# A decoder block with two cross attentions: row products 22 slots ahead over three banks, turned maxima in single precision, and a last stage that centres x in PSUM by ScalarE

## The reference

```
x = x + tanh(g_xattn[0]) * wkv(layernorm(x), context)                 # a recurrence
x = x + tanh(g_ffn[0])   * one-bit feed-forward(layernorm(x))         # 512 -> 2048 -> 512
x = x + tanh(g_xattn[1]) * attention(layernorm(x), context)           # 16 heads of 32
x = x + tanh(g_ffn[1])   * ternary projection(layernorm(x))           # RMS norm, int8 activations
```

```
q = qdq(x) @ qdq(wq).T + bq ;  k, v = split(context @ wkv.T + bkv)
attn = softmax(q k^T / sqrt(32)) ;  o = attn v ;  out = qdq(o) @ qdq(wp).T + bp
```

## Time and profile before

| what | value |
|---|---|
| median of 3 runs | 1025.7 us (1024.91 to 1027.72) |
| the profiled execution | 1025.1 us, span 1023.4 us |
| PE busy | 832.3 us, 81% |
| DVE busy | 794.2 us, 78% |
| ACT busy | 560.1 us, 55% |
| POOL busy | 489.6 us, 48% |
| attention, first to last score product | 624.6 to 899.8 us |

### The profile page before, as it was taken

How to read it: one execution, slowest core, us unless ns; L and a number is a source line. 1 busy time by engine, 2 the same in 40 slices (tenths; PEclk the granted TensorE clock), 3 DMA queues, 4 the chain that set the end, 5 groups by cost and what they waited for, 6 DMA issues and landing times.

```text
span 1023.4 us, 15702 instructions
## 1 busy us (share of the span) xinstructions
PE 832.3 (81%) x4423; PEld 362.5 (35%) x4423; DVE 794.2 (78%) x1524; ACT 560.1 (55%) x993; POOL 489.6 (48%) x556
## 2 busy tenths in 40 slices
PE   1289889828999999999999956989989898854554
PEld 1245445403444454444454421222222222222221
DVE  3949899857898999998998655677777778427995
ACT  2358888734455565665655543555555555544441
POOL 1185665212344443445433444475756666536561
PEclk9569999969999999999999957999999999977776
DMA  8538987622333323233233331212122120000111
GB/s 283 190 96 217 220 205 200 179 57 42 62 73 62 62 52 62 52 71 62 51 62 63 72 96 40 75 51 71 55 62 64 56 68 2 1 0 9 53 41 61
DMA packets 165159, 84.45 MB, mean 83 GB/s; under 512 B 116960, under 2 KB 149872, under 8 KB 165104
## 3 DMA queue, kind: packets, MB, share of 16 engines
q1 hardware_dynamic: 165104, 83.81, 32.5%
HBM read 37.50 MB, written 12.58 MB: 49 GB/s over the span
## 4 chain that ended last, share of the span: by engine, by line
PE 50%; DVE 15%; issue 6%; SPq 3%; ACT 3%; POOL 1%; DMA 0%; DVEq 0%; ACTq 0%; POOLq 0%
PE bank L1002 20%; PE bank L1011 10%; PE bank L1099 5%; DVE B L1529 4%; PE bank L1072 4%; PE bank L1089 4%; SPq L412 3%; PE bank L1109 2%; ACT A L852 1%; DVE B L1536 1%; PE bank L1111 1%; DVE B L1622 1%; PE bank L1029 1%; DVE B L1624 1%; POOL B L609 1%
## 5 line engine op out<-in xcount | busy, mean ns | idle before, releaser
L1002 PE MATMUL bank<-A,B 128*128 128x512 f16 x1024 | 233.0, 381 | 18.6 <-DMA B<-B 14.8
L1529 DVE TENSOR_REDUCE B<-bank 128x1 f32<-128x512 f32 x256 | 163.5, 685 | 71.2 <-PE bank L1072 69.9
L852 ACT ACTIVATE A<-bank 128x512 f32<-128x512 f32 x256 | 138.8, 592 | 88.7 <-PE bank L1089 86.3
L525 POOL TENSOR_TENSOR B<-B 128x512 f16<-128x512 f32 x64 | 75.5, 1179 | 207.1 <-ACT B L740 154.2
L1002 PEld LDWEIGHTS bank<-A,B 128*128 128x128 f16 x1024 | 100.3, 98 | 141.5 <-issue 18.3
L598 POOL TENSOR_TENSOR B<-A 128x512 f32<-128x512 f32 x64 | 79.3, 1268 | 112.8 <-ACT A L852 112.8
L1011 PE MATMUL bank<-A,B 128*128 128x512 f16 x512 | 120.7, 379 | 0.0
L1072 PE MATMUL bank<-A 96*128 96x512 f16 x256 | 100.9, 405 | 15.3 <-DVE B L1529 10.3
L735 ACT ACTIVATE bank<-B 128x512 f32<-128x512 f32 x64 | 38.5, 602 | 124.2 <-DVE B L1424 123.9
L1089 PE MATMUL bank<-A 98*128 98x512 f16 x256 | 96.5, 391 | 11.3 <-DMA A<-B 6.6
L598 POOL TENSOR_TENSOR B<-B,A 128x512 f32<-128x512 f32 x64 | 79.1, 1269 | 0.0
(11 more groups left out here) (232 smaller groups left out, 1546.5 us busy)
## 6 DMA issues: line engine op xcount, KB each, us to landing
B<-in_L_ffn_w_dram SPq DMA_DIRECT2D x48, 256.0 KB, 3.5
A<-k_parts SPq DMA_DIRECT2D x48, 128.0 KB, 2.5
A<-B SPq DMA_DIRECT2D x192, 32.0 KB, 1.9
X<-in_x_dram SPq DMA_DIRECT2D x4, 1024.0 KB, 13.6
B<-in_ctx_dram SPq DMA_DIRECT2D x16, 256.0 KB, 5.3
k_parts<-B SPq DMA_DIRECT2D x16, 256.0 KB, 4.7
v_rows<-B SPq DMA_DIRECT2D x16, 256.0 KB, 3.2
B<-v_rows SPq DMA_DIRECT2D x16, 256.0 KB, 3.2
```

What stands on the lines that cost most here:

```text
L525: nc.gpsimd.tensor_tensor(HLb[j][:, 1, :], Db[j % 2], HLb[j][:, 0, :], ALU.subtract).then_inc(lo_done, 1)
L852: nc.scalar.activation(PR[(HG * t + j) % 8], bank[2 + j % 2][:, :], ACT.Exp, scale=SCALE).then_inc(exp_done, 1)
L1002: last = mm(bank[2 * n + q][:, :], XQT[a][:, m, :], wt[:, m % DB, j * 512:j * 512 + 512], start=(m == 0), stop=(m == 2 * DB - 1))
L1529: reduce(NMX[:, t, j:j + 1], bank[n % 2][:, :], AX.X, ALU.max, negate=True).then_inc(row_max, 1)
```

## The change

In the attention:

- Row products run 22 slots ahead of the scores instead of one group (`LEAD` 6 more), over three banks 0, 1 and 5 instead of two. The list `ROWS` says how many stand in each slot, and `coming` which ones. Before the first group 22 of them run instead of 16.
- The maxima are turned in single precision straight from `NMX` (now two buffers) into 4 rows of bank 4, so `max_parts` goes. ACT's copy makes the high half-precision part in `CT[0]`, and a new DVE operation `c_low` takes bank 4 minus that for the low part `CT[1]`. `send_c` waits for both.
- `c_turn` moves from the middle of slots 12 to 15 to slot 9, ACT's `c_out` to after exponential 10, `c_low` to slot 12 of DVE's list.
- `sums_out` moves from DVE to ACT, after exponential 5. `ot_out` moves from before exponential 0 to after exponential 3. `sum_weights` is cut in two: the four products over the last block of exponentials (`sum_last`) come first, in slot 2, those over `ACC` in slot 3. `sum_turn` is in slot 6, `o_turn` in slot 7 and now into bank 7.
- PE and DVE have all four batches written out instead of a loop over the middle ones.

In the last stage:

- ACT writes mean minus x into banks 6 and 7, one operation per block, and DVE multiplies that with gamma (a tensor by tensor operation in place of L1622); the sign is put right in L1628's place. The two operations L1625 and L1626 become one for each of two columns.
- ACT rounds the attention output of unit s+1 in step s, after L879, where it rounded unit s at the head of step s. ACT's steps are all written out.
- Maxima of the last four blocks are taken one by one, and the scales of the first 12 blocks are computed before the last group is normalized.

```diff
-        NMX = part(16, F32, "p (t j) -> p t j", t=TB)
-        NHL = part(32, F16, "p (t h j) -> p t h j", t=TB, h=2)
-        CT = part(512, F16)
+        NMX = [part(16, F32, "p (t j) -> p t j", t=TB) for _ in range(2)]
+        CT = [part(512, F16) for _ in range(2)]
...
+        ROWS = (1, 1, 2, 2, 1, 1, 1, 1, 1, 1, 1, 0, 1, 1, 1, 0)
+        LEAD = 6
+        ROW_BANKS = (0, 1, 5)
+
+        def coming(b, g):
+
+            at, slots = 16 * (DB * b + g + 1) + LEAD, []
+            for count in ROWS:
+                slots.append([divmod(r, 16) for r in range(at, at + count) if r < 16 * DB * BATCH])
+                at += count
+            return slots
...
                 sp.wait_ge(ct_ready, b * DB + g + 1)
+                sp.wait_ge(ct_low, b * DB + g + 1)
                 for h in range(2):
-                    sp.dma_start(QS[96 + h:97 + h, HG * g:HG * g + HG, :], CT[HG * h:HG * h + HG, :]).then_inc(c_in, 16)
+                    sp.dma_start(QS[96 + h:97 + h, HG * g:HG * g + HG, :], CT[h][0:HG, :]).then_inc(c_in, 16)
...
+                            if (t, j) == (0, 3) and not opening:
+                                ot_out(*preceding(b, g))
+                            if (t, j) == (1, 1) and not opening:
+                                sums_out(*preceding(b, g))
+                            if (t, j) == (2, 2) and not closing:
+                                c_out(*following(b, g))
...
+                if live(s - 2):
+
+                    act.wait_ge(st4, s - 1)
+                    up_to(act, zs_ready, s - 2)
+                    for t in range(2):
+                        row = X[:, bass.ds((s - 2) * 2 + t, 1), :].rearrange("p a d -> p (a d)")
+                        last = nc.scalar.activation(bank[6 + t][:, :], row, ACT.Identity, bias=mv1[:, t, 0:1], scale=-1.0)
+                    last.then_inc(centred, 1)
...
-                up_to(pe, row_max, (b * DB + g) * 16 + n - 1)
-                mm(bank[n % 2][:, :], QS[0:96, HG * g + j, t * P:t * P + P], KS[0:96, HG * g + j, :],
+                up_to(pe, row_max, r - 2)
+                mm(bank[ROW_BANKS[r % 3]][:, :], QS[0:96, HG * g + j, t * P:t * P + P], KS[0:96, HG * g + j, :],
...
-                    last_ = turn(bank16[4][0:8, t * P:t * P + P], NHL[:, t, :, :].rearrange("p h j -> p (h j)"), id16[:, :])
+                    last_ = turn(bank[4][0:HG, t * P:t * P + P], NMX[g % 2][:, t, :], id32[:, :])
...
-            ORDER = ("r r r v r a s r s r s s",
-                     "r s r s v r s r s r o d",
-                     "r s r s v r s r s r",
-                     "s s v c s s")
...
+                    for slot in range(16):
+                        t, j = slot // HG, slot % HG
+                        for at, n in ahead[slot]:
+                            rows(at // DB, at % DB, n)
+                        scores(b, g, t, j)
+                        if j == 1 and t > 0:
+                            weigh(b, g, t - 1)
+                        if slot == 1 and not opening:
+                            weigh(*preceding(b, g), TB - 1)
+                        if slot == 2 and not opening:
+                            sum_last(*preceding(b, g))
+                        if slot == 3 and not opening:
+                            sum_weights(*preceding(b, g))
+                        if slot == 6 and not opening:
+                            sum_turn(*preceding(b, g))
+                        if slot == 7 and not opening:
+                            o_turn(*preceding(b, g))
+                        if slot == 9 and not closing:
+                            c_turn(*following(b, g))
...
+            def c_low(b, g):
+
                 n = b * DB + g
+                dve.wait_ge(ct_ready, n + 1)
+                up_to(dve, c_in, n * 32)
+                tt(CT[1][0:HG, :], bank[4][0:HG, :], CT[0][0:HG, :], ALU.subtract).then_inc(ct_low, 1)
...
+                dve.wait_ge(centred, u + 1)
                 for t in range(2):
-                    last_ = stt(Z[:, t, :], row(u, t), mv1[:, t, 0:1], gam_all[:, :], ALU.subtract, ALU.mult)
+                    last_ = tt(Z[:, t, :], bank[6 + t][:, :], gam_all[:, :], ALU.mult)
                 link(last_)
                 link(reduce(ZM, Z, AX.X, ALU.max, apply_absolute_value=True))
-                link(tt(ZAM, ZM, FR, ALU.mult))
-                link(ts(ZAM, ZAM, 1e-5, None, ALU.add))
+                for t in range(2):
+                    last_ = ts(ZAM[:, t:t + 1], ZM[:, t:t + 1], FR[:, t:t + 1], 1e-5, ALU.mult, ALU.add)
+                link(last_)
                 link(recip(ZR, ZAM))
-                stt(ZR, ZR, 127.0, FR, ALU.mult, ALU.mult).then_inc(zs_ready, 1)
+                stt(ZR, ZR, -127.0, FR, ALU.mult, ALU.mult).then_inc(zs_ready, 1)
```

More of the change, by code:

```diff
@@ L826, in c_out @@
                 up_to(act, c_in, n * 32)
-                nc.scalar.copy(CT[0:8, :], bank16[4][0:8, 0:512]).then_inc(ct_ready, 1)
+                nc.scalar.copy(CT[0][0:HG, :], bank[4][0:HG, :]).then_inc(ct_ready, 1)
             def ot_out(b, g):
@@ L886, in _ @@
             act.wait_ge(osc_ready, 1)
-            pipeline(act, out_step)
+            o_round(0)
+            for s in range(UNITS + LAG):
+                out_step(s, lambda u: 0 <= u < UNITS)
         @block.tensor
@@ L1142, in attend @@
                     opening, closing = first and g == 0, last and g == DB - 1
[L1143 to L1161 removed]
+                    ahead = coming(b, g)
+                    for slot in range(16):
[17 more added lines that the diff above has]
+                            c_turn(*following(b, g))
             pe.wait_ge(down_read, TOK)
@@ L1167, in _ @@
                 rows(0, 0, n)
+            for n in range(LEAD):
+                rows(0, 1, n)
             pe.wait_ge(ks_ones, 1)
             c_turn(0, 0)
-            batches(pe, attend)
+            for b in range(BATCH):
+                attend(b, b == 0, b == BATCH - 1)
             weigh(BATCH - 1, DB - 1, TB - 1)
+            sum_last(BATCH - 1, DB - 1)
             sum_weights(BATCH - 1, DB - 1)
+            sum_turn(BATCH - 1, DB - 1, True)
             o_turn(BATCH - 1, DB - 1)
-            sum_turn(BATCH - 1, DB - 1, True)
             pe.wait_ge(row_max, 16 * DB * BATCH)
@@ L1580, in _, with scales @@
                 maxima(0, 0, n)
-            max_parts(0, 0)
-            attend(0, True, False)
-            with dve.Fori(1, BATCH - 1) as b:
-                step.turn(DB, b - 1)
-                attend(b, False, False)
-            step.turns_over(BATCH - 2)
-            attend(BATCH - 1, False, True)
-            sums_out(BATCH - 1, DB - 1)
+            for n in range(LEAD):
+                maxima(0, 1, n)
+            c_low(0, 0)
+            for b in range(BATCH):
+                attend(b, b == 0, b == BATCH - 1)
+            def scales(n, m):
+                link(ts(OSC[:, n:m], OM[:, n:m], 1.0 / 127.0, 1e-8, ALU.mult, ALU.max))
+                link(recip(OR[:, n:m], OSC[:, n:m]))
+                ts(OST[:, n:m], OSC[:, n:m], TG[:, 1:2], None, ALU.mult).then_inc(osc_ready, 1)
+            link(nc.vector.memset(held[:, 2:3], 0.0))
+            scales(0, TOK - TB)
             invert_sums(BATCH - 1, DB - 1)
@@ L1658, in _ @@
             with dve.Fori(LAG, UNITS) as s:
-                step.turn(8, s - LAG)
+                step.turn(7, s - LAG)
                 out_step(s, lambda u: True)
```

114 lines of the change are left out of this document (50 added, 64 removed).

## The result

The changed kernel takes 993.6 us (median of 4 runs, 988.19 to 998.05) beside 1026.7 us for the kernel before in the same session: a ratio of 0.968 with an interval of 0.965 to 0.971. The forecast was 997.0, range 982 to 1013. The profiled execution of after took 988.19 us, span 986.4, which is 36.9 us less than that of before.

| | before | after | difference | forecast |
|---|---|---|---|---|
| start of the span to the first score product | 624.6 | 618.3 | -6.3 | 0 |
| first score product to the first integers of the last stage | 286.4 | 266.5 | -19.9 | -20.9 |
| first integers to the end | 112.4 | 101.6 | -10.8 | -7.4 |
| one attention group in the middle | 17.55 | 16.39 | -1.16 | -1.2 |
| one middle step of the last stage | 11.64 | 10.14 | -1.50 | -1.05 |

What follows compares the result with a forecast made beforehand. PE waits for DVE's maxima and split bound the attention group, and DVE the last stage. Savings of 19.0 + 1.05 + 0.85 + 7.4 = 28.3 us from 1025.1 gave 996.8, so 997 us, range 982 to 1013.

Steps and rivals of the forecast that it cites:

- The layout: Middle attention group laid out from single durations: ACT's chain and the bias row both end near 16.3 us, 1.2 less.
- Rival (1): Attention group: ACT's copies hide, the bias comes sooner, PE alone bounds it at 15.2 us; total 981; 15%.
- (2): Attention group: bias row late through a `c_low` wait and DMAs behind query loads; 17.3 us, total 1011; 25% with (4).
- (3): Attention: score 0 waits for the row sent after `c_out` and `c_low`, making the kernel slower, up to 1030 us; 7%.
- Rival (4): Attention: row products are ahead but PE stops for something else; group stays 17.5 us, total 1013; 25% with (2).
- with three banks a product needs the maximum three back: Attention row products: the third bank means they no longer wait, as DVE needs only 12.4 us a group.
- the prediction's opening: Attention group: some 3 us of PE waits, for DVE's maxima and its split, which the change takes away.
- The ends: Attention's first and last groups and after: last add 19.0 us earlier, then 1.05 and 0.85 us less.
- 8.35 as the start of `z_add`: Last stage: L1638 starts at 8.35 instead of 9.39 us, held by PE's projection; 1.05 us less a step, 7.4 over seven.
- PE at its higher level: Last stage: upper bound with PE at its higher level and no wait, a step 1.9 us shorter.
- The centring at nothing: Last stage: ACT's centring, 2 x 0.60 us, costs nothing, covered by the 1.17 us of POOL's power.
- the small ones at 6.4: Last stage: DVE's small operations after the maximum end 6.4 us into the step, the maximum at 5.9.

Runs made afterwards that it cites:

- the two experiments: Changed kernel with the old half-precision split and turn: 1022.7 us, group 17.7 to 19.1; kernel before with the single-precision turn alone: 1023.8 us, group 17.55.
- the second pair: Unedited changed kernel and kernel before run once more: medians 994.5 and 1026.0 us, ratio 0.970.
- the last version: Changed kernel with turn, ACT's copy, `c_low` and the inversion of the sums each moved one place earlier: 989.4 us, ratio to before 0.9625.

## Why the prediction was right, point by point

- **The group, 16.3 against 16.39.** The layout held in each of the marks read above within 0.1 us, except that the query loads took 7.80 us and not 8.80, so the queue had 1.9 us in hand and not 0.9. The turn took 0.53 us on the chain and not 0.44. Rival (1), PE alone, fell since ACT and the bias row do bind: taking the row away left 16.29. Rivals (2) and (3) fell since `c_low` met no wait (0.68 in all 16) and the queue was free. Rival (4) did not happen here; the new order with the split beside POOL's adds behaves as it says, row products ahead and PE stopped by something else, with a group of 17.7 and more.
- **Right number, part of the reason wrong.** The step "with three banks a product needs the maximum three back" gave the bank a part that it doesn't have: two banks give the same 16.39. What removes the waits is the lead and the order, since a row product then asks for a maximum that is long done. Nor do the two gains of the attention add up as the prediction's opening let a reader think (waits for the maxima, and the split): each alone, placed as in the two experiments, is worth nothing.
- **The ends.** The first group took 14.54 (14.5 laid out), the last 15.3 from score 0 to the last add (15.0), which came 259.3 us after the first score and not 258.3. The copy of the sums followed 1.56 later (1.15), the first integers 5.62 after that (6.06). Added up, 19.9 instead of 20.9. The 1.15 was 1.05 off two halves' 2.21; the one half that is left costs more than half of that.
- **The last stage, 10.8 against 7.4, is the mis-sized term.** The wait for POOL was where and as long as I put it, to 7.97 (7.95). But I took 8.35 as the start of `z_add`, from PE's projection at 3.60 us, and in a shorter step it took 2.89, done 7.3 us in. PE did not take over; L1683 started at 7.91, the step fell by 1.50, and seven of them make 10.5. The duration from the trace of before was the duration at a granted clock of 0.50, and I carried it over as if it were the work's own; in the same trace the block took 2.64 in another step. The bound "PE at its higher level" stood in the prediction, and the truth lay between. At a clock of 0.50 the term would have stood: there the addition came at 8.54. The gain of this stage goes with the clock, 10.8 and 10.5 us in the two executions of after, 9.9 in the last version with the same code (112.4 - 102.5).
- **The centring at nothing** held: ACT's two took 1.30 us and ended 0.09 us behind POOL's power. Of the step's gain it is 0.83 us; the other 0.67 is the small operations by single columns, which the prediction has in "the small ones at 6.4" without naming them as a gain.
- **The sum, 996.8 against 993.6.** That the total came within 3.4 us is in part luck: the attention gave 1.0 less than forecast and the last stage 3.4 more. The terms measured are 30.7 us (31.2 in the second pair) against 28.3 forecast; the 6.3 us ahead of the change are not the change's.

## What to carry to other kernels

Lay a group out by hand from single durations, and list every chain that ends at the same instruction: where two end within 0.1 us, moving one does nothing, and the version that won moved turn, copy and subtraction together. A small VectorE operation beside long GpSimd work can cost what is left of the GpSimd instruction, whatever its own size (1.08 us for 0.17 of work); here an operand in PSUM (0.68 us beside the adds as without) or single columns (0.33 for two) avoided it. A row's releaser is the last event, not always the cause: compare the distance to the producer with a kernel in which nothing else is in question. Before taking a matmul block's duration into a new schedule, look at the granted clock under which it was read.

## What the runs showed that I had not expected

- Of two small forms on the same data, one waits for GpSimd and the other doesn't: with two columns 1.48 us (L1673), as two operations of one column 0.33 in all, beside the same POOL add. A `tensor_scalar` on 12 columns took 1.30 us while POOL added, and 0.17 on 4 columns when it rested; the lines are L1626 in the timeline of after:

```profile
871.43 1.30 DVE L1626 TENSOR_SCALAR B<-B 128x12 f32<-128x12 f32 x1
...
884.23 0.17 DVE L1626 TENSOR_SCALAR B<-B 128x4 f32<-128x4 f32 x1
```

- The step of the last stage is not a property of its code alone. With the same lines it was 10.14 us where PE's projection ran at 0.65, and 10.25 where it ran at 0.54; POOL's wait and PE's projection lie so close that the clock decides which of them ends last.
- The same split of the maxima cost 1.37 us in before and 2.3 us in another slot, by nothing but where it fell between POOL's adds.
- Untouched stages differ by 6.3 us between two executions of one kernel (618.3 and 624.6 to the same instruction), a fifth of what the change is worth. Without a second execution this would have been read as a gain.
